# The next-to-last router's columns on VectorE, and that batch's scatters set around four small operations of the last batch

## The chip, the cores and the metric

The kernel runs on one core of one Trainium2 chip. The metric is the device time of that core in microseconds (us), as the median of several executions; lower is better. The engines are TensorE (PE, with its weight loads shown apart as PEld), VectorE (DVE), ScalarE (ACT), GpSimd (POOL) and SyncE (SP), which only issues transfers here. Each engine works through its own list of instructions in order, and they meet through semaphores: counters that one engine raises and another waits on.

## The reference

One transformer layer in fp32 on 8 batches of 512 tokens with 256 channels: attention, then a mixture of experts. Cut to what matters:

```python
x = x + attention(layernorm(x))          # 16 query heads, 4 key heads of 16, rope, causal
h = layernorm(x)                         # 4096 tokens
logits = h @ gate_w.T                    # 64 experts
topv, topi = jax.lax.top_k(logits, 8)
rw = softmax(topv)
gu = einsum('nh,eih->nei', h, gu_w);  gate, up = split(gu)
out = einsum('nei,ehi->nh', silu(gate) * up * W, dp_w)      # W holds rw at topi
out = out + sigmoid(h @ sh_gate1_w.T) * ((silu(h @ sh_gate_w.T) * (h @ sh_up_w.T)) @ sh_down_w.T)
x = x + out
```

## The kernel before, in words

The program has two phases. In the first, attention runs batch by batch, and each batch's tokens are routed and sent ("scattered") to the rows of a DRAM tensor `rows_d`, where every expert owns whole blocks of 128 rows. In the second, 320 such blocks are loaded (`xg<-rows_d`), put through their expert, scattered back to `res_d`, and summed per token. SP loads the first block only after all scatters of all batches have landed.

A batch is `b = h * 2 + par`, 0 to 7, and has four tiles of 128 tokens. The first phase is written as beats of 40 slots (`beat`, below); a beat holds the score and softmax work of one batch (`main`, eight units of five slots), and beside it work of its neighbours, each step put at a slot number. The slots only fix the order of the instructions in every engine's list: an engine that is early runs ahead until a semaphore stops it. The pieces around the change are:

- **`post`**, per tile: the attention output is turned, normalised by the softmax sums, projected, added to x, and its mean and variance are taken on DVE (L910, `mv`). At its step 2 POOL makes the reciprocal square root of the variance in two operations (L439 and L441, `rstd`), which the headline of the change calls a deviation. At step 4 DVE applies it (L916, `pay`), and then PE, ACT and DVE make logits and the top eight (L923 to L929).
- **`route`**, per batch, steps 0 to 11: counts of tokens per expert on PE, small column arithmetic on `col` (64 by 16) and the final row numbers `slot_i` (L322). The column arithmetic is `route_columns`: 3 instructions at step 0, 6 at step 2, one at step 4, 8 at step 5 and one at step 11, 19 in all. 12 of them are `chained`: the engine waits for its own result before it goes on. POOL runs them for batches 0 to 6, DVE for batch 7, the last. PE waits for `diag` (L310) before it makes the ranks (L668 to L678).
- **`scatter`**, per batch 32 times: one indirect transfer, issued by POOL (L457), that writes one row of 272 numbers for each of 128 tokens. The first one of a batch waits for `slot_i` and for the blank rows.
- **`ending(h, par, n)`** is true for the last n batches, two where n is left out.

The last three beats are: batch 7's main, beside which batch 6 goes through `post` and, at slots 29 to 39, through route steps 0 to 10, while batch 5's 32 scatters stand at slots 13 to 39; then a beat without main, in which batch 6's step 11 stands at slot 0, its scatters at slots 1 to 32, the end of batch 7's attention at slots 0 to 10, batch 7's `post` at slots 11 to 21 (its four deviations at slots 13 to 16) and its route from slot 22; then a beat with batch 7's step 11 and scatters. In the trace these are roughly 640 to 700 us, 700 to 760 us and 760 to 802 us.

## Time and profile before

| | |
|---|---|
| median of 3 executions | 1388.26 us (1385.78 to 1390.83) |
| the profiled execution, its own time | 1382.82 us |
| its span in the trace | 1381.0 us |
| busy share PE, DVE, ACT, POOL | 79%, 51%, 48%, 52% |
| mean granted TensorE clock | 0.903 of full |
| last scatter of the first phase ends | 801.9 us |

Times in the trace are microseconds from the start of its span. A row of a timeline gives the start, the busy time, the engine, the line of the kernel, the operation, what it writes and reads, how many instructions were merged, and in brackets how long the engine had been idle and what released it. "Remote" as the releaser means that no operation ended just then whose semaphore would explain it. "Issue" is time in which the engine waited for nothing that the profile shows. The names of line numbers are those of the kernel before; those of the changed kernel are 3 higher from L259 on.

### The profile page before, as it was taken

How to read it: one execution, taken by the hardware profiler on the slowest of the kernel's cores; microseconds unless marked ns; L12 is line 12 of the kernel's file. 1: busy time of each engine (PE TensorE's matmuls, PEld its weight loads, DVE VectorE, ACT ScalarE, POOL GpSimd, SP SyncE). 2: the span in 40 equal slices, each digit the busy share in tenths (PEclk: the TensorE clock that was granted, in tenths of full speed). 3: DMA queues.
4: the chain of work that ended last, by engine and by line, in shares of the span. 5: the costliest groups of instructions: out<-in, count | busy, mean ns of one | idle time of the engine just before them, and what ended most of it. 6: DMA issues, size and time to landing. Idle time of an engine off the chain costs nothing.

```text
span 1381.0 us, 24099 instructions
## 1 busy us (share of the span) xinstructions
PE 1085.1 (79%) x7306; PEld 835.8 (61%) x7306; DVE 708.3 (51%) x2229; ACT 661.8 (48%) x1650; POOL 722.3 (52%) x954
## 2 busy tenths in 40 slices
PE   3798998888888888889765068888879788788775
PEld 1566666655666656656533057777767677777663
DVE  3466766575666756666515411212244454544456
ACT  2466655555555555654421034544444454545441
POOL 3111225746557474564566745655556565565552
PEclk9699999899999999999867579989989999999996
DMA  2587876212122121231229765555767777766535
GB/s 82 174 283 226 279 253 230 99 39 101 63 70 107 39 97 57 66 104 61 84 85 314 252 191 168 170 161 158 233 218 275 262 274 239 273 237 216 199 108 207
DMA packets 142300, 233.22 MB, mean 169 GB/s; under 512 B 17287, under 2 KB 119894, under 8 KB 136800
## 3 DMA queue, kind: packets, MB, share of 16 engines
q1 hardware_dynamic: 67360, 101.06, 22.9%
q0 software_dynamic: 27648, 69.28, 14.1%
q10 hardware_dynamic: 47168, 61.35, 13.4%
q8 instruction: 63, 1.03, 0.3%
q14 instruction: 61, 0.50, 0.1%
HBM read 107.32 MB, written 132.66 MB: 174 GB/s over the span
## 4 chain that ended last, share of the span: by engine, by line
PE 47%; DVE 16%; another core or an unknown queue 14%; issue 11%; ACT 5%; POOL 3%; DMA 2%; ACTq 0%; DVEq 0%; SPq 0%; POOLq 0%
PE psB L1369 8%; PE psD L1386 6%; DVE nmax L866 6%; PE psv L601 4%; PE psA L1359 4%; PE ps L505 4%; PE ps L552 3%; PE psp L498 3%; PE psp L484 3%; PE ps L512 3%; PE psC L1377 2%; DMA x_d<-oT 2%; DVE acc L1201 1%; PE psq L628 1%
## 5 line engine op out<-in xcount | busy, mean ns | idle before, releaser
L1447 POOL DMA_INDIRECT res_d<-y,dst_i x320 | 322.6, 1008 | 230.5 <-ACT y L1275 127.6
L457 POOL DMA_INDIRECT rows_d<-pay,slot_i x256 | 256.2, 1001 | 76.0 <-issue 74.1
L866 DVE TENSOR_REDUCE nmax<-ps 128x1 f32<-128x512 f32 (+3 forms) x448 | 226.0, 531 | 132.2 <-PE ps L512 88.8
L732 ACT ACTIVATE wgu_s<-ps 128x512 f32<-128x512 f32 x320 | 191.9, 600 | 121.5 <-PE ps L512 90.2
L1178 DVE TENSOR_TENSOR inner<-inner,psB 128x128 f32<-128x128 f32 x160 | 45.9, 287 | 302.4 <-ACT inner L1262 221.8
L1369 PE MATMUL psB<-wgu_s,xT 128*128 x1280 | 182.4, 288 | 18.9 <-ACT xT L1255 12.3
L1386 PE MATMUL psD<-wdp_s,innerT 128*128 x640 | 176.5, 399 | 13.0 <-issue 7.6
L1369 PEld LDWEIGHTS psB<-wgu_s,xT 128*128 128x128 f32 x1280 | 166.1, 203 | 24.9 <-issue 24.8
L512 PE MATMUL ps<-mask,ident_b 128*128 128x256 bf16 (+1 forms) x640 | 174.7, 273 | 0.0
L505 PE MATMUL ps<-kT,qT 96*128 96x512 f32 (+3 forms) x512 | 168.2, 391 | 6.5 <-DVE nmax L866 3.3
L552 PE MATMUL ps<-qT,kT 128*128 128x512 f32 (+3 forms) x512 | 164.8, 385 | 4.5 <-ACT wgu_s L732 3.9
L1255 ACT COPY xT<-psA 128x512 f32<-128x512 f32 x160 | 97.1, 607 | 142.8 <-PE psA L1359 90.5
L1359 PE MATMUL psA<-cst,xg 128*128 128x128 f32 x640 | 104.0, 284 | 59.5 <-DMA xg<-rows_d 52.8
L1386 PEld LDWEIGHTS psD<-wdp_s,innerT 128*128 128x128 f32 x640 | 114.5, 200 | 29.9 <-issue 20.4
L1275 ACT COPY y<-psD 128x512 f32<-128x512 f32 x160 | 98.4, 615 | 68.3 <-remote 40.4
L1359 PEld LDWEIGHTS psA<-cst,xg 128*128 128x128 f32 x640 | 80.1, 148 | 61.4 <-DMA xg<-rows_d 53.7
L505 PEld LDWEIGHTS ps<-kT,qT 96*128 96x128 f32 x512 | 89.1, 203 | 32.2 <-DVE nmax L866 15.3
L512 PEld LDWEIGHTS ps<-mask,ident_b 128*128 128x128 bf16 x640 | 64.2, 100 | 64.7 <-issue 34.0
L1201 DVE SCALAR_TENSOR_TENSOR acc<-yk,rw_all,acc 128x256 f32<-128x256 f32 x204 | 98.8, 485 | 4.4
L1262 ACT ACTIVATE inner<-psB 128x128 f32<-128x128 f32 x160 | 48.4, 303 | 100.1 <-remote 66.5
L552 PEld LDWEIGHTS ps<-qT,kT 128*128 128x128 f32 x512 | 91.2, 205 | 7.4 <-ACT wgu_s L732 4.2
L601 PE MATMUL psv<-wgu_s 128*32 128x512 f32 (+3 forms) x1024 | 89.8, 470 | 3.7 <-issue 2.6
(257 smaller groups left out, 1606.3 us busy)
## 6 DMA issues: line engine op xcount, KB each, us to landing
rows_d<-blank ACTq DMA_DIRECT2D x8, 5440.0 KB, 19.3
xg<-rows_d SPq DMA_DIRECT2D x160, 272.0 KB
yk<-res_d SPq DMA_DIRECT2D x30, 1024.0 KB, 5.8
wgu_s<-wgu_in ACTq DMA_DIRECT2D x8, 1024.0 KB
x_d<-x SPq DMA_DIRECT2D x30, 192.5 KB
xs<-x_d SPq DMA_DIRECT2D x30, 192.5 KB
res_d<-y,dst_i POOLq DMA_INDIRECT x320
wgu_s<-x_in SPq DMA_DIRECT2D x32, 128.0 KB, 2.1
```

The costliest lines, as they stand in the source:

```text
L457: pool.indirect_dma_start(rows_d, bass.IndirectOffsetOnAxis(ap=slot_i[par][:, t, k:k + 1], axis=0), pay[par][:, t, :], None).then_inc(s_sc ...
L505: pe.matmul(ps1[:, bank, at:at + keys], qT[par][0:96, p, i * P:(i + 1) * P], kT[par][0:96, 2 * (p // 2) + ab, 0:keys], start=(at == 0), st ...
L512: return pe.matmul(blocks, ident_b[:], mask[:].unsqueeze(1).to_broadcast([P, blocks.shape[1], P]), start=False, stop=True, skip_group_chec ...
L552: pe.matmul(ps2[:, bank, at:at + n], kT[par][:, 2 * (p // 2) + ab, kt * P:(kt + 1) * P], qT[par][:, p, kt * P:SEQ], start=(at == 0), stop= ...
L601: last = pe.matmul(psv[32 * hh:32 * hh + 32, kt * P:SEQ], v1[par][:, kt, g, :], rhs, start=(kt == 0), stop=(kt == TILES - 1), skip_group_c ...
L732: act.activation(pexp[p % 4][:, s, :], ps2[:, (5 * p + s) % 2, :], ACT.Exp, scale=HEAD_D ** -0.5).then_inc(s_exp, 1)
L866: return dve.tensor_reduce(nmax[u][:, tile, heads[0]:heads[-1] + 1], src, AX.X, ALU.max, negate=True)
L1201: dve.scalar_tensor_tensor(out=acc[:, u], in0=yk_at(tile)[:, k], scalar=rw_all[:, at:at + 1], in1=xs_at(tile)[:, 0:D] if k == 0 else acc[: ...
L1359: last = pe.transpose(psA[:, i % 2, (b * KC + c) * P:(b * KC + c + 1) * P], xg[:, (2 * i + b) % G, c * P:(c + 1) * P], ident)
L1369: last = pe.matmul(psB[:, i % 2, b * GU:(b + 1) * GU], xT[:, i % A, b, c, :], wgu_s[:, bass.ds(off + c * GU, GU)], start=(c == 0), stop=(c ...
L1386: last = pe.matmul(psD[:, i % 2, b * D:(b + 1) * D], innerT[:, i % A, b, :], wdp_s[:, bass.ds(off, D)], start=True, stop=True)
L1447: pool.indirect_dma_start(res_d, bass.IndirectOffsetOnAxis(ap=dst_i[:, j % (2 * G):j % (2 * G) + 1], axis=0), y[:, j % Y, :], None, bounds ...
```

## The change

Two edits. The route columns of batch 6 go from POOL's list to DVE's, at the same slots (steps 0, 2, 5 and 11 ahead of what DVE already had there, step 4 behind it). And in the beat without main, batch 6's 32 scatters no longer stand one at each of the slots 1 to 32: twelve stand at slots 1 to 12, and twenty from slot 18 to slot 34, so that none stands at slots 13 to 17.

```diff
                     for n in range(TILES * TOP):
-                        if late and slot == first + n * spread // (TILES * TOP):
+                        at = first + n * spread // (TILES * TOP)
+                        if routed and behind:
+                            at = 1 + n if n < 12 else 18 + (n - 12) * 17 // (TILES * TOP - 12)
+                        if late and slot == at:
                             steps["scatter"](h - 1, par, n)
...
                 def route(h, par, k):
-                    if not ending(h, par, 1):
+                    if not ending(h, par):
                         route_columns(pool, h, par, k)
...
-                    if ending(h, par, 1) and k in (0, 2, 5, 11):
+                    if ending(h, par) and k in (0, 2, 5, 11):
                         route_columns(dve, h, par, k)
...
-                        if ending(h, par, 1):
+                        if ending(h, par):
                             route_columns(dve, h, par, k)
```

POOL's list before, from the end of batch 6's route columns to the end of the first phase (L457 is a scatter, L439 and L441 a deviation; the first seven scatters are batch 5's, and the last 48 are 16 of batch 6 and 32 of batch 7):

```order
L318 COPY col<-col 64x1
L457 DMA rows_d<-pay,slot_i 40960x272 x7
L322 TENSOR_SCALAR slot_i<-slot_f 128x32
L457 DMA rows_d<-pay,slot_i 40960x272 x13
L439 TENSOR_SCALAR rstd<-mv 128x1
L441 TENSOR_TENSOR rstd<-rstd,minus_half 128x1
L457 DMA rows_d<-pay,slot_i 40960x272
L439 TENSOR_SCALAR rstd<-mv 128x1
L441 TENSOR_TENSOR rstd<-rstd,minus_half 128x1
L457 DMA rows_d<-pay,slot_i 40960x272
```

POOL's list after, the same place (L460 is the scatter, L442 and L444 the deviation), from the last deviation of batch 6:

```order
L442 TENSOR_SCALAR rstd<-mv 128x1
L444 TENSOR_TENSOR rstd<-rstd,minus_half 128x1
L460 DMA rows_d<-pay,slot_i 40960x272 x32
L442 TENSOR_SCALAR rstd<-mv 128x1
L444 TENSOR_TENSOR rstd<-rstd,minus_half 128x1
L442 TENSOR_SCALAR rstd<-mv 128x1
L444 TENSOR_TENSOR rstd<-rstd,minus_half 128x1
L442 TENSOR_SCALAR rstd<-mv 128x1
L444 TENSOR_TENSOR rstd<-rstd,minus_half 128x1
L442 TENSOR_SCALAR rstd<-mv 128x1
L444 TENSOR_TENSOR rstd<-rstd,minus_half 128x1
L460 DMA rows_d<-pay,slot_i 40960x272 x52
```

Between batch 6's last deviation and batch 7's first, POOL now has 32 scatters in one row and nothing else: the last 20 of batch 5 and the first 12 of batch 6. Behind the four deviations stand 52, which are 20 of batch 6 and the 32 of batch 7; before, 3 stood between the deviations and 48 behind them.

DVE's list before, in the seventh unit of batch 7's main (L866 is a row maximum of the scores, L938 to L949 the parts of batch 6's route that DVE had):

```order
L938 TENSOR_TENSOR col<-psq,col 64x1
L866 TENSOR_REDUCE nmax<-ps 128x1
L941 TENSOR_REDUCE esum<-etop 128x4
L944 RECIPROCAL erec<-esum 128x4
L866 TENSOR_REDUCE nmax<-ps 128x1 x3
L947 TENSOR_TENSOR col<-psq,col 64x1
L949 TENSOR_TENSOR col<-psq,col 64x1
L866 TENSOR_REDUCE nmax<-ps 128x1 x2
L866 TENSOR_REDUCE nmax<-ps 128x2
```

And after, the later part of the same unit (L869 is the row maximum):

```order
L869 TENSOR_REDUCE nmax<-ps 128x1 x2
L311 TENSOR_TENSOR col<-col 64x1
L312 TENSOR_TENSOR col<-col 64x1
L313 TENSOR_TENSOR diag<-cst,col 64x192
L317 TENSOR_TENSOR col<-col 64x1
L318 TENSOR_SCALAR col<-col 64x1
L319 TENSOR_TENSOR col<-col 64x1
L320 COPY col<-col 64x1
L321 COPY col<-col 64x1
L869 TENSOR_REDUCE nmax<-ps 128x2
```

Eight instructions of the columns now stand ahead of that unit's last maximum. Six more stand behind the same unit's first maximum, three ahead of the last maximum of the unit before, one behind L952 (step 4), and one (step 11) behind all of batch 7's maxima.

## Rows read from the trace of the kernel before

**Rows 1.** The page's first line, and the chain that ended last: start, us, what
```profile
span 1381.0 us, 24099 instructions
...
711.14 12.04 another core or an unknown queue
...
803.47 2.50 DMA xg<-rows_d
```

**Rows 2.** Timelines of PE and ACT, end of batch 7's attention
```profile
691.71 0.48 PE L668 MATMUL psq<-diag,ones_f 64*128 64x128 f32 x2 [2.33 <-POOL diag L310]
...
704.42 0.59 ACT L759 COPY oT<-psv 128x512 f32<-128x512 f32 x1 [4.73 <-remote]
...
711.76 4.50 PE L601 MATMUL psv<-wgu_s 128*32 128x512 f32 x32 [0.69 <-ACT wgu_s L732]
...
723.21 0.59 ACT L759 COPY oT<-psv 128x512 f32<-128x512 f32 x1 [11.49 <-remote]
```

**Rows 3.** Timeline of POOL, 667 to 704 us: batch 5's scatters and batch 6's columns
```profile
667.81 1.09 POOL L457 DMA_INDIRECT rows_d<-pay,slot_i  x1 [0.19 <-issue]
...
679.85 0.97 POOL L457 DMA_INDIRECT rows_d<-pay,slot_i  x1 [0.30 <-issue]
683.65 0.19 POOL L295 TENSOR_SCALAR col<-col 64x1 f32<-64x1 f32 x1 [2.83 <-DVE col L938]
...
693.23 0.18 POOL L318 COPY col<-col 64x1 f32<-64x1 f32 x1 [0.16 <-POOL col L317]
694.22 1.26 POOL L457 DMA_INDIRECT rows_d<-pay,slot_i  x1 [0.81 <-POOL col L318]
...
703.12 0.34 POOL L322 TENSOR_SCALAR slot_i<-slot_f 128x32 int32<-128x32 f32 x1
```

**Rows 4.** Timeline of DVE, 678 to 700 us: batch 7's row maxima
```profile
678.60 0.76 DVE L866 TENSOR_REDUCE nmax<-ps 128x1 f32<-128x384 f32 x2 [4.36 <-remote]
682.29 0.69 DVE L866 TENSOR_REDUCE nmax<-ps 128x2 f32<-128x512 f32 x1 [2.94 <-remote]
...
699.72 0.17 DVE L881 TENSOR_TENSOR mt<-nmax,mt 128x8 fp32r<-128x8 f32 x1
```

**Rows 5.** Timeline of POOL, 704 to 801 us: the scatters of batches 6 and 7
```profile
704.62 1.06 POOL L457 DMA_INDIRECT rows_d<-pay,slot_i  x1 [1.16 <-issue]
...
720.01 0.97 POOL L457 DMA_INDIRECT rows_d<-pay,slot_i  x1 [0.30 <-issue]
730.41 0.22 POOL L439 TENSOR_SCALAR rstd<-mv 128x1 f32<-128x1 f32 x1 [9.42 <-DVE mv L910]
...
737.51 0.57 POOL L441 TENSOR_TENSOR rstd<-rstd,minus_half 128x1 f32<-128x1 f32 x1
738.27 1.22 POOL L457 DMA_INDIRECT rows_d<-pay,slot_i  x1 [0.19 <-issue]
...
757.75 0.96 POOL L457 DMA_INDIRECT rows_d<-pay,slot_i  x1 [0.30 <-issue]
761.66 0.96 POOL L457 DMA_INDIRECT rows_d<-pay,slot_i  x1 [2.95 <-issue]
...
800.96 0.96 POOL L457 DMA_INDIRECT rows_d<-pay,slot_i  x1 [0.30 <-issue]
```

**Rows 6.** Timeline of DVE, 735 to 760 us: batch 7's post and route
```profile
735.16 0.18 DVE L910 BATCH_NORM_AGGREGATE mv<-stat 128x2 f32<-128x6 f32 x1
...
738.12 0.41 DVE L916 TENSOR_SCALAR pay<-oT,mv,rstd 128x256 f32<-128x256 f32 x1 [1.93 <-POOL rstd L441]
...
744.00 0.15 DVE L297 TENSOR_SCALAR col<-col 64x1 f32<-64x1 f32 x1
744.30 0.15 DVE L298 TENSOR_TENSOR col<-col 64x1 f32<-64x1 f32 x1
744.38 0.20 DVE L299 TENSOR_SCALAR col<-col 64x1 f32<-64x1 f32 x1
...
759.26 0.18 DVE L322 TENSOR_SCALAR slot_i<-slot_f 128x32 int32<-128x32 f32 x1 [2.92 <-remote]
```

## The prediction

> **What bounds the kernel now.** I read the page first, then the chain that ended last, then the timelines of single engines around the place of the change. The span is 1381.0 us [rows 1]; the profiled execution took 1382.82 us and the median is 1388.26, so I add what the change does to the span onto both. The changed lists differ only from 676 us on and up to the end of the first phase, where the first expert block is loaded at 803.47 [rows 1]. All work behind that load is the same and starts when the last scatter has landed, so the change is worth what it does to the end of POOL's 32 scatters of batch 7, whose last one starts at 800.96 [rows 5]. They run at a fixed pace: 31 steps from 761.66 to 800.96 are 1.27 us each [rows 5]. So the question is when the first of them starts, now 761.66.
>
> Back from there: POOL finishes batch 6's scatters at 757.75 + 0.96 = 758.71, then takes 2.95 us to start batch 7's first [rows 5]. About 1.16 of that is POOL going through the waits of a batch's first scatter, as at 704.62 [rows 5]; the other 1.8 are a real wait for `slot_i`, which DVE makes at 759.26 [rows 6]. That comes from DVE's chain of batch 7's post, which starts when ACT copies the last attention output at 723.21, after 11.49 us without work [rows 2]. This is the largest idle piece, and the chain shows it as 12.04 us without a known cause [rows 1]: PE's products began at 711.76 and the modelled end is 716.26, yet ACT is released 7 us later [rows 2].
>
> The rows show a pattern for it. POOL issues 13 scatters without a pause from 704.62 to 720.98 [rows 5], and ACT is released 2.2 us after the last. The previous copy waited 4.73 us and was released at 704.42 [rows 2], 1.3 us after POOL ended a row of seven scatters at 703.1 [rows 3]. DVE's maxima at 678.60 and 682.29 waited 4.36 and 2.94 us [rows 4], the second until 1.5 us after the scatter of 679.85 to 680.82, behind which POOL paused [rows 3]. In each case a finished operation's signal reaches the waiting engine late while scatters run back to back, and soon after they stop. I take that as the working reading: **long unbroken rows of scatters hold up the signals of the other engines**. The trace doesn't show why.
>
> **The columns leave POOL.** In 667 to 703 us POOL had pauses in which it waited for DVE's and PE's parts of the route, for instance the 2.83 us before 683.65 and the stretch from 683.65 to 693.23 [rows 3]. With the 19 instructions gone, nothing stands between batch 5's scatters: the order shows 20 of batch 5 in one row from 667.81 [rows 3]. They end at 667.81 + 19 x 1.27 + 0.96 = 692.9 instead of 703.1. That by itself gains nothing, since the next scatter waits for batch 6's `slot_i`, which is now DVE's. But it makes one unbroken row of 25 us where there were pauses.
>
> **The columns arrive at DVE**, among batch 7's maxima. On DVE a chained step takes 0.30 us (744.00 to 744.30) and one without a wait 0.08 (744.30 to 744.38) [rows 6]. 12 x 0.30 + 7 x 0.1 = 4.3 us. Of it some hides in DVE's waits for PE between maxima; bounds 0 and 4.3, and I take half, 2.2, as nothing speaks for either end. The Trainium skill (VectorE: DVE Perf Modes, Rules for kernel authors) says to "minimize op *count*, not sems", because the pipeline empties after each operation anyway. By it the waits would be free and 19 operations of 0.15 to 0.20 us would cost about 3.3; the two pitches above contradict it, a wait costs 0.2 us here, and the sum goes by the rows. On the other side PE no longer waits 2.33 us for POOL's `diag` at 691.71 [rows 2], because DVE makes it two slots ahead; I take the 2.3 off.
>
> Ten slots of maxima lie between 682.29 and 699.72 [rows 4]: 17.4 us, without the 2.3 it is 15.1, with DVE's 2.2 it is 17.3, 1.73 a slot. Under a row of scatters the two slots before took from 674.24 (678.60 less its wait) to 682.29, 4.0 each [rows 4]. Now the row goes on to 692.9, and signals are held to about 694.2. That is 11.9 us at 4.0, three slots. The other seven take 12.1, so the maxima end at 706.3 and not 699.9: **6.4 us later**. Bounds: nothing held, 699.6; nothing moves at all until 694.2, 711.5.
>
> **Batch 6's `slot_i` and its first twelve.** POOL made `slot_i` at 703.12 [rows 3], after its seven scatters; DVE now makes it at 706.4. The first scatter starts 1.5 us behind that start, as 704.62 behind 703.12, at 707.9, and the twelfth ends 11 x 1.27 + 0.96 = 14.9 later, at 722.8. Batch 7's last products need, from 699.9 to their modelled end at 716.26, 16.4 us of which about 4 were held (the 4.73 of [rows 2]); so they are done near 718.7. Their signal is held until the twelve are through, plus 1.3 to 2.2 as measured above: 724.1 to 725.0. ACT's copy moves from 723.2 to about 724.5, **1.3 later**. So the shift of 6.4 is mostly absorbed, because the old row of 13 ended at 721.0 and the new row of 12 ends at 722.8.
>
> **The four deviations kept clear.** The last mean and variance is ready at 735.16 + 0.18 = 735.34, and POOL's deviation for it ended at 737.51 + 0.57 = 738.08, behind interleaved scatters; DVE waited 1.93 us for it at 738.12 [rows 5, 6]. Without them it takes 0.2 + 0.9 us, so it ends at 736.4, and DVE's chain and `slot_i` come up to 1.7 earlier. But POOL then has 20 scatters of batch 6 left, where it had 16: they end at 736.6 + 19 x 1.27 + 0.96 = 761.7, against 758.71 [rows 5]. `slot_i` (near 757.6) is then waiting for POOL and not POOL for it. Batch 7's first scatter starts at 761.7 + 1.16 = 762.9, **1.2 later** than 761.66. POOL's 9.42 us of idleness before 730.41 [rows 5] stays unused, and one more scatter than before is on its wrong side. Bounds: 1.2, and 3.0 if `slot_i`'s signal is itself held to the end of the row, as at 759.26 (2.92 us, [rows 6]), when the old gap of 2.95 returns.
>
> Sum: 1.3 + 1.2 = +2.5 us. The profiled execution would take 1385.3, the median 1388.26 + 2.5 = **1390.8**.
>
> **Rivals.** (a) *Nothing is held during the 20.* The first 7 us of the row from 704.62 passed without a hold, as the products could begin at 711.76 [rows 2, 5], so a long row need not hold always. Then the maxima end at 699.6, the twelve scatters run from about 701.2 to 716.1, ACT's copy comes at 717.4 to 718.3, 5.3 earlier, and with the 1.2 the total is -4.1: 1384.2. Against it stand the waits of [rows 4] under only ten scatters. (b) *The maxima are late but the last products' signal is not held*, since they end at 718.7 in the middle of a row: -4.5 + 1.2 = -3.3, 1385.0. Against it stand both copies of [rows 2]. (c) *Slower: under the 20 almost nothing moves.* DVE now waits for its own results 12 times inside the row, and each can be caught like the 2.92 us before 759.26 [rows 6]. The maxima end at 711.5, the twelve run from 713.1 to 728.0, the copy comes at 729.3 to 730.2, 6.5 later, and with 1.2 to 3.0 the total is +7.7 to +9.5: 1396 to 1398. Since batch 6's scatters start from DVE, each us by which the maxima end beyond 706.3 costs one; it becomes visible when they end later than about 708. (d) *The second edit does what it says and is worth its 1.7 us:* only if POOL is through before `slot_i` comes, and 736.6 + 25.1 against 757.6 says it isn't; where copy and post come early, all of this moves together.
>
> **How the numbers follow.** Chances: the forecast 0.50, (a) 0.20, (b) 0.12, (c) 0.18. A measurement of this kernel can tell about 0.3%, 4.2 us, from no change. The forecast lies inside it, but its bounds (the hold, and the 3.0) put 0.08 of its 0.50 beyond; (c) is beyond, slower; of (a) half is beyond, faster, and of (b) a sixth. Faster 0.15, within 0.59, slower 0.26. The range takes in (a) and (b) with some scatter below, and (c) but for its far end: 1383.5 to 1397.
>
> **What would show it.** After: batch 5's scatters end near 693; batch 7's maxima end near 706, with DVE waits of 2 to 5 us marked remote before 694; DVE's `slot_i` for batch 6 directly behind; ACT's last copy within 1 to 2 us after the twelfth scatter; no wait of DVE for `rstd`; 52 scatters behind the deviations with only some 1.2 us between the 20th and the 21st; the first block loaded near 806. If the maxima end near 700 and the copy comes near 718, (a) is right; if they end beyond 710, (c). The prediction is wrong in kind if ACT's copy isn't tied to the end of the scatters, or if POOL waits for batch 7's `slot_i` again.

## The result, and the profile after

The changed kernel takes 1401.13 us (median of 6 executions, 1395.51 to 1405.85), the kernel before takes 1387.16 beside it (6 executions, 1380.30 to 1390.83). The ratio is 1.0094, with a 95% interval of 1.0067 to 1.0120: **0.9% slower**, where I had forecast 0.2%, inside what can be told from no change, and a range up to 1397.0. The profiled execution took 1400.32 us with a span of 1398.5, against 1382.82 and 1381.0 [rows 1]. One execution of all that are reported here, of 1677.67 us at a granted clock of 0.554 in experiment 12, was in a slower state of the chip and is left out of its ratio.

The first lines that answer to [rows 1]: the page's first line, then from the chain that ended last (start, us, what) the piece that is longest in the disputed stretch, and the load of the first expert block.

```profile
span 1398.5 us, 24099 instructions
...
682.45 15.21 another core or an unknown queue
...
819.32 2.66 DMA xg<-rows_d
```

The load starts 15.85 us later than at 803.47 [rows 1], so nearly all of the 17.5 us of the span arise before it. The timeline of POOL (start, us, engine, line, operation, what is written from what, and in brackets the idle time before it and who ended it) shows the rows of scatters. Every row starts or ends with one of these lines; left out are scatters at the same pitch and the four deviations.

```profile
669.93 1.09 POOL L460 DMA_INDIRECT rows_d<-pay,slot_i  x1 [0.19 <-issue]
...
694.09 0.96 POOL L460 DMA_INDIRECT rows_d<-pay,slot_i  x1 [0.30 <-issue]
716.67 0.96 POOL L460 DMA_INDIRECT rows_d<-pay,slot_i  x1 [21.61 <-issue]
...
730.58 0.96 POOL L460 DMA_INDIRECT rows_d<-pay,slot_i  x1 [0.30 <-issue]
...
748.05 1.09 POOL L460 DMA_INDIRECT rows_d<-pay,slot_i  x1 [0.18 <-issue]
...
772.18 0.96 POOL L460 DMA_INDIRECT rows_d<-pay,slot_i  x1 [0.30 <-issue]
777.61 0.96 POOL L460 DMA_INDIRECT rows_d<-pay,slot_i  x1 [4.46 <-issue]
```

The row of twenty of batch 5 starts at 669.93, where the kernel before had 667.81 [rows 3]: at this point, ahead of anything that the change touches, this execution is already 2.1 us late. I take that off below. The rows of scatters are as forecast: twenty in 25.1 us, twelve in 14.9, twenty in 25.1. What is not as forecast is what the other engines do under them. DVE, from the first row of twenty to batch 7's `slot_i`:

```profile
681.42 0.75 DVE L869 TENSOR_REDUCE nmax<-ps 128x1 f32<-128x384 f32 x2 [5.05 <-remote]
...
697.69 0.69 DVE L869 TENSOR_REDUCE nmax<-ps 128x2 f32<-128x512 f32 x1 [15.24 <-remote]
...
699.37 0.14 DVE L298 TENSOR_SCALAR col<-col 64x1 f32<-64x1 f32 x1
699.65 0.15 DVE L299 TENSOR_SCALAR col<-col 64x1 f32<-64x1 f32 x1
...
715.21 0.17 DVE L884 TENSOR_TENSOR mt<-nmax,mt 128x8 fp32r<-128x8 f32 x1
715.33 0.18 DVE L325 TENSOR_SCALAR slot_i<-slot_f 128x32 int32<-128x32 f32 x1
...
747.90 0.47 DVE L919 TENSOR_SCALAR pay<-oT,mv,rstd 128x256 f32<-128x256 f32 x1 [0.46 <-POOL rstd L444]
...
761.84 0.15 DVE L319 TENSOR_TENSOR col<-col 64x1 f32<-64x1 f32 x1 [1.19 <-DVE col L318]
...
770.49 0.42 DVE L969 TENSOR_TENSOR place<-psq,thd 128x256 f32<-128x256 f32 x1 [4.60 <-issue]
...
775.90 0.18 DVE L325 TENSOR_SCALAR slot_i<-slot_f 128x32 int32<-128x32 f32 x1 [2.86 <-remote]
```

And ACT at the same three places: an exponential under the first row, the last attention output behind the twelve, and batch 7's route under the second row of twenty.

```profile
698.39 0.60 ACT L735 ACTIVATE wgu_s<-ps 128x512 f32<-128x512 f32 x1 [14.91 <-PE ps L515]
...
733.76 0.59 ACT L762 COPY oT<-psv 128x512 f32<-128x512 f32 x1 [11.75 <-remote]
...
770.19 0.27 ACT L800 COPY thd<-psq 128x128 f32<-128x128 f32 x1 [16.21 <-remote]
```

The waits of 4.36 and 2.94 us of [rows 4] have become 5.05 and 15.24. The second stands until 2.6 us after the row's last scatter ends (694.09 + 0.96 = 695.05), and ACT stands still over the same time. PE's timeline under the row (xcount is the number of matmuls in a line), and at its end the products of batch 7's last attention step:

```profile
681.95 0.44 PE L515 MATMUL ps<-mask,ident_b 128*128 128x256 bf16 x1
...
682.88 2.36 PE L604 MATMUL psv<-wgu_s 128*32 128x384 f32 x16
...
688.47 0.48 PE L604 MATMUL psv<-wgu_s 128*32 128x128 f32 x2 [1.82 <-issue]
689.90 0.37 PE L604 MATMUL psv<-wgu_s 128*32 128x128 f32 x1 [0.95 <-issue]
691.30 0.44 PE L604 MATMUL psv<-wgu_s 128*32 128x128 f32 x2 [1.03 <-issue]
692.73 0.37 PE L604 MATMUL psv<-wgu_s 128*32 128x128 f32 x1 [0.99 <-issue]
694.14 0.78 PE L508 MATMUL ps<-kT,qT 96*128 96x512 f32 x1 [1.04 <-issue]
...
722.06 2.36 PE L604 MATMUL psv<-wgu_s 128*32 128x512 f32 x32 [0.69 <-issue]
```

Two different things can be seen here.

**The work is done and its signal comes late.** The maximum at 697.69 waits for one product alone, the one at 681.95, whose modelled end is 682.39: 15.3 us pass between the two. ACT's exponential at 698.39 waits for a product with the modelled end 682.95. ACT's last copy waits for the products that start at 722.06 and have the modelled end 724.42; it is at 733.76, 2.2 us after the last of the twelve, as that of 723.21 [rows 2] came 2.2 us after the thirteenth. The trace also records the updates of the semaphores. The one of those last products is recorded at 733.74, directly ahead of the copy, so the delay lies ahead of the update, and not between the update and ACT.

**PE crawls.** The 24 products from 682.88 on are one group, and the kernel has no wait ahead of any of them. Yet from the seventeenth on they come one or two at a time every 0.7 to 2.1 us, 10.2 us for all (682.88 to 693.10), with idle time marked "issue". I had read only DVE, ACT and POOL at such places before. So "signals are held" is half of it: **under the long row an engine's own instructions can come slowly too**. But DVE's and ACT's waits here aren't that crawl, since the products that they need stand ahead of the 24.

Between 753.98 and 770.19 ACT waits again, for a product whose modelled end is 762.62. Before that, DVE is slow in batch 7's route: a step that had a pitch of 0.30 us at 699.37 has an idle time of 1.19 ahead of it at 761.84. Each of these steps waits for the signal of DVE's own step before.

### The profile page after: what moved, and what is told of

The parts are those of the page before. It is cut to its first block, busy times and chain, and to the rows that moved or that the text cites. A ratio compares the mean times of both kernels' runs of the same rounds, so it can differ in the third digit from the quotient of the medians.

```text
span 1398.5 us, 24099 instructions
## 1 busy us (share of the span) xinstructions
PE 1095.6 (78%) x7306; PEld 844.4 (60%) x7306; DVE 711.2 (51%) x2248; ACT 663.9 (47%) x1650; POOL 715.6 (51%) x935
## 3 DMA queue, kind: packets, MB, share of 16 engines
q0 software_dynamic: 27648, 69.28, 13.9%
q10 hardware_dynamic: 47168, 61.35, 13.3%
## 4 chain that ended last, share of the span: by engine, by line
PE 52%; DVE 16%; issue 14%; another core or an unknown queue 11%; ACT 3%; POOL 2%; DMA 1%; SPq 0%; ACTq 0%; DVEq 0%; POOLq 0%
PE psB L1372 9%; PE psD L1389 7%; DVE nmax L869 6%; PE psA L1362 4%; PE psv L604 4%; PE ps L508 3%; PE ps L555 3%; PE psp L501 3%; PE psp L487 3%; PE psC L1380 3%; PE ps L515 3%; PE psq L631 1%; PE ps L549 1%; DVE acc L1204 1%
## 5 line engine op out<-in xcount | busy, mean ns | idle before, releaser
L460 POOL DMA_INDIRECT rows_d<-pay,slot_i x256 | 253.8, 992 | 97.6 <-issue 97.3
L869 DVE TENSOR_REDUCE nmax<-ps 128x1 f32<-128x512 f32 (+3 forms) x448 | 225.5, 530 | 146.5 <-PE ps L515 88.0
L1372 PE MATMUL psB<-wgu_s,xT 128*128 x1280 | 185.1, 291 | 15.3 <-issue 8.6
L1389 PE MATMUL psD<-wdp_s,innerT 128*128 x640 | 179.0, 402 | 17.3 <-ACT innerT L1271 8.2
L1389 PEld LDWEIGHTS psD<-wdp_s,innerT 128*128 128x128 f32 x640 | 116.4, 203 | 35.4 <-issue 25.7
L515 PEld LDWEIGHTS ps<-mask,ident_b 128*128 128x128 bf16 x640 | 64.1, 100 | 64.9 <-issue 36.5
```

Of the source, the lines that this page charges most:

```text
L460: pool.indirect_dma_start(rows_d, bass.IndirectOffsetOnAxis(ap=slot_i[par][:, t, k:k + 1], axis=0), pay[par][:, t, :], None).then_inc(s_sc ...
L515: return pe.matmul(blocks, ident_b[:], mask[:].unsqueeze(1).to_broadcast([P, blocks.shape[1], P]), start=False, stop=True, skip_group_chec ...
L869: return dve.tensor_reduce(nmax[u][:, tile, heads[0]:heads[-1] + 1], src, AX.X, ALU.max, negate=True)
L1372: last = pe.matmul(psB[:, i % 2, b * GU:(b + 1) * GU], xT[:, i % A, b, c, :], wgu_s[:, bass.ds(off + c * GU, GU)], start=(c == 0), stop=(c ...
L1389: last = pe.matmul(psD[:, i % 2, b * D:(b + 1) * D], innerT[:, i % A, b, :], wdp_s[:, bass.ds(off, D)], start=True, stop=True)
```

## Experiments

**The theories.** Theory 1 is the working reading of the prediction: a long unbroken row of POOL's scatters holds up the other engines (their signals, as I put it; by the rows above their instructions too), and the change made such rows. Theory 2: the harm is the work that DVE got, 19 operations with 12 waits on itself among the maxima. Theory 3, in the first two experiments: the second edit made the loss. Ratios are always to the kernel before, run in between on the same chip. They aren't the quotients of the medians. Each run bears the number of its chip: experiments 1 to 4 ran on chip 0 (kernel before 1389.52 us), 5, 6, 8 and the first kernel of 9 on chip 5 (1366.53), the second run of the changed kernel, 7, 10 and the second kernel of 9 on chip 8 (1365.60), 11 on chip 1 (1211.39) and 12 on chip 11 (1212.16). The chip of the result above (1387.16) isn't on record. Times of different chips can't be compared, ratios can with care; chips 1 and 11 turned out to matter by themselves, and I call them the quick chips.

**1. The columns alone.** The kernel before, with one condition changed at its three places:

```diff
-                    if not ending(h, par, 1):
+                    if not ending(h, par):
```

> The first edit alone: batch 6's columns on DVE, the scatters at their old slots. Theory 1 (the unbroken row of 20 scatters holds up the other engines' signals while batch 7's maxima run): DVE has one wait of over 10 us inside that row, the maxima end some 13 us later than before, and the kernel is 7 to 12 us slower than before. Theory 2 (DVE's added work and its own waits among the maxima cost it): the same time, but without a wait of over 5 us; the delay lies in the slots that hold the columns. Theory 3 (the second edit made the loss, by 20 scatters behind the deviations): within 3 us of before.

Measured: 1399.35 us, 1.0079 (1.0043 to 1.0116). DVE in this kernel, under a row of twenty from 668.81 to 693.9:

```profile
679.66 0.76 DVE L866 TENSOR_REDUCE nmax<-ps 128x1 f32<-128x384 f32 x2 [4.41 <-remote]
...
697.28 0.69 DVE L866 TENSOR_REDUCE nmax<-ps 128x2 f32<-128x512 f32 x1 [16.56 <-remote]
```

The first edit alone gives most of the loss and the same hold as the changed kernel: the maximum's product has its modelled end at 680.52, 16.8 us ahead of 697.28.

**2. The scatters' slots alone.** The kernel before with the other edit:

```diff
+                        if routed and behind:
+                            at = 1 + n if n < 12 else 18 + (n - 12) * 17 // (TILES * TOP - 12)
```

> The second edit alone: the columns stay on POOL, twelve scatters of batch 6 ahead of the four deviations and 20 behind. In the changed kernel the stretch from ACT's last copy of the attention output to the end of the last scatter grew by 5.3 us. Theory 1: this is the second row of 20 holding batch 7's route, so this kernel is 3 to 6 us slower than before. Theory 2: only POOL's later end counts, +1.2 us. Theory 3: 10 us slower or more.

Measured: 1389.86 us, 1.0024 (0.9990 to 1.0059). There is no row of twenty among the maxima, but 52 scatters now stand in one row from 742.89 to 808.74, and under it ACT's copy for the route waits:

```profile
761.45 0.27 ACT L800 COPY thd<-psq 128x128 f32<-128x128 f32 x1 [12.62 <-remote]
```

What the second edit costs is too small to be told from nothing by the interval. The stretch from ACT's last copy to batch 7's first scatter, which grew by 5.4 us in the changed kernel, is 40.38 us here and 38.45 in the kernel before. That is 1.9 more, not the 5.3 that theory 1 was given.

**3. The columns on DVE, POOL's waits kept.** Edit 1, and POOL goes through batch 6's waits for the route as before, without doing the arithmetic. That keeps pauses between its scatters.

```diff
+                    elif not ending(h, par, 1):
+                        for at, sem_, count in ((0, s_top, 4 * (b + 1)), (2, s_cnt, b + 1), (4, s_erec, b + 1),
+                                                (5, s_base, b + 1), (5, s_pool, 12 * (b + 1)), (11, s_slot, b + 1)):
+                            if k == at:
+                                pool.wait_ge(sem_, count)
...
```

> As cols_only, but POOL keeps the waits of batch 6's route (for the top eights, the counts, the reciprocal sums, the bases, the end of the columns and the slots) at their old places, without the arithmetic; so batch 5's scatters have pauses again while DVE does exactly the work of cols_only. Theory 1: no row of 20, no wait of over 6 us, within 4 us of before. Theory 2: as slow as cols_only, since DVE's list is the same.

Measured: 1391.78 us, 1.0032 (1.0000 to 1.0063). DVE's list is that of experiment 1. Its waits at the disputed place are near those of the kernel before again, 3.65 and 3.23 us. But the pauses now end where DVE is quick, and 7 scatters of batch 5 and 13 of batch 6 stand in one row from 699.39 to 724.71:

```profile
684.62 0.76 DVE L873 TENSOR_REDUCE nmax<-ps 128x1 f32<-128x384 f32 x2 [3.65 <-remote]
689.01 0.69 DVE L873 TENSOR_REDUCE nmax<-ps 128x2 f32<-128x512 f32 x1 [3.23 <-remote]
```

```profile
723.62 0.59 ACT L766 COPY oT<-psv 128x512 f32<-128x512 f32 x1 [17.16 <-remote]
```

Theory 1 had expected no wait over 6 us; with the new row there is one all the same. The hold went with the row, not with the work: from DVE's maxima to ACT's copy.

**4. The changed kernel, its scatters paced.** In batch 7's main part POOL waits, ahead of each scatter, for the maxima of two slots before its own:

```diff
+                            if PACED(h, par, main):
+                                steps["pace"](h, par, slot)
...
+                def pace(h, par, slot):
+                    pool.wait_ge(s_red, 5 * PAIRS_OF_HEADS * (h * 2 + par) + slot - 1)
```

> The changed kernel with one thing more: in the beat with batch 7's main, each scatter of POOL first waits for the row maxima of two slots before, so that POOL can't run ahead of DVE and stops when DVE stops. Theory 1: POOL's stopping ends each hold, no DVE wait of over 5 us there, the maxima end 8 us or more sooner than in the changed kernel, and the total is 3 to 7 us over before (the second edit's share stays). Theory 2: as slow as the changed kernel, 12 to 14 us over before, since DVE's list is the same and POOL's is later.

Measured: 1390.36 us, 1.0017 (0.9987 to 1.0046). The row of twenty is now one of ten, one of two, one of six and two single ones; the longest remote wait of DVE there is 4.32 us. From the start of batch 5's twenty scatters to the end of the maxima it takes 35.4 us (677.48 to 712.92), where the changed kernel has 45.5 and the kernel before 32.1. Most of the loss is gone, with all of DVE's new work in place. The row of twenty behind the deviations is still there, and ACT still waits 22.05 us for it at 773.14.

**5. DVE's work alone.** The kernel before, in which DVE does 19 spare operations of the same kinds, with the same chain of 12 waits on itself, at the same places, while POOL does its own as before. Three of them are smaller than those of the change, as the expectation says. A part of one of the five pieces:

```diff
+                if k == 2:
+                    chained(eng.tensor_scalar(c(5), c(4), P / 2 - 0.5, 1.0 / P, ALU.add, ALU.mult), 1)
+                    chained(eng.tensor_scalar(c(5), c(5), 1.0, None, ALU.add), 2)
+                    chained(eng.tensor_scalar(c(6), c(5), 1.0, 0.5, ALU.add, ALU.mult), 3)
+                    eng.tensor_tensor(c(7), c(6), c(1), ALU.subtract)
...
```

> The kernel before, and beside it 19 operations of the kind and order of the columns on DVE, at the places where the change puts them, on spare tiles with their own chain of 12 waits (the wide one writes 64 by 128 bf16 instead of 64 by 192 fp32, and two of the three small ones bf16); nobody waits for them, and POOL's list is the old one. It prices DVE's added work alone. Theory 1: at most 4 us slower than before, most likely 1 to 3. Theory 2 (DVE's work is what costs): 8 us or more slower.

Measured: 1366.39 us, 1.0016 (0.9992 to 1.0040). The upper end is 5.5 us, the middle 2.2, and nothing at all lies inside the interval too (the quotient of the medians is 0.9999). Theory 2 can't give the 0.9% of the change.

**6. The changed kernel with pauses.** Ahead of batch 5's scatters 12, 16, 20, 24 and 28 POOL does five chained memsets of a spare tile, 2.5 us in all from the end of one scatter to the start of the next.

```diff
+                    if isinstance(b, int) and b == BATCH - 3 and n >= 12 and n % 4 == 0:
+                        for again in range(5):
+                            pool.memset(spare[:], 0.0).then_inc(s_spare, 1)
+                            pool.wait_ge(s_spare, 5 * (n // 4 - 3) + again + 1)
...
```

> The changed kernel, with five pauses of POOL of some 2 us each in the row of 20 scatters (ahead of batch 5's scatters 12, 16, 20, 24 and 28), made of five small memsets of a spare tile, so by time alone and not by a wait for another engine. Theory 1 in the form that a pause of POOL ends a hold: no hold over 8 us in that row, the maxima end 5 us or more sooner than in the changed kernel, total 3 to 9 us over before. If holds need more than a pause, or what counts is the number of scatters in some longer time, the hold stays near 15 us and so does the loss.

Measured: 1364.13 us, 0.9982 (0.9957 to 1.0007). **POOL does more, and the kernel is faster.** I had expected 3 to 9 us over the kernel before, and it is not slower at all. In the rows of four no wait of DVE is above 1.4 us and none of ACT above 3.0. The changed kernel without pauses once more, now on chip 8, whose kernel before takes 1365.60 us against the 1366.53 of chip 5:

> The changed kernel once more, beside the next three on one chip. Both theories: 1.006 to 1.012 times the kernel before, POOL's row of 20 scatters, DVE's wait of about 15 us inside it, maxima ending 8 to 10 us late.

Measured: 1379.28 us, 1.0084 (1.0051 to 1.0118). Against that the pauses give back 1.0%, all of the 0.84% that was lost; the comparison is between two chips, each with its own kernel before. Its DVE and ACT under the row of twenty (663.27 to 688.42):

```profile
687.40 0.69 DVE L869 TENSOR_REDUCE nmax<-ps 128x2 f32<-128x512 f32 x1 [12.93 <-remote]
691.88 0.69 DVE L869 TENSOR_REDUCE nmax<-ps 128x1 f32<-128x512 f32 x1 [3.22 <-remote]
```

```profile
690.92 0.60 ACT L735 ACTIVATE wgu_s<-ps 128x512 f32<-128x512 f32 x1 [15.60 <-remote]
```

Here PE's 24 products are through at 682.32, and the product that the maximum of 687.40 waits for has its modelled end at 675.67, 11.7 us ahead of it. From ACT's last copy to batch 7's first scatter it is 39.59 us in this execution, where the one above has 43.85.

**7. Rows of eight.** The same with pauses ahead of scatters 12, 20 and 28 only (`n in (12, 20, 28)`), on chip 8 as well.

> The changed kernel with three pauses, before batch 5's scatters 12, 20 and 28, so rows of eight where rows of four gave 0.9982. If the hold grows with the length of the row from about the fifth scatter on: two waits of DVE or ACT of 3 to 6 us, one in each row of eight, and 1.001 to 1.004. If only rows of 10 and more hold: no wait above 2.5 us there and the 0.998 of the rows of four. If the harm is DVE's work: 1.006 or more, whatever the rows.

Measured: 1365.70 us, 0.9994 (0.9968 to 1.0019). The first row of eight, 661.48 to 671.42, has a wait; the second, 673.87 to 683.69, has none on DVE above 1.4 us:

```profile
672.87 0.69 DVE L876 TENSOR_REDUCE nmax<-ps 128x2 f32<-128x512 f32 x1 [6.09 <-PE ps L522]
679.55 0.76 DVE L876 TENSOR_REDUCE nmax<-ps 128x1 f32<-128x384 f32 x2 [1.17 <-PE ps L522]
```

So eight in a row can hold up DVE, and need not. I had expected a hold in each, or in none. The name of the releaser is PE's matmul here and not "remote", but the end of the wait, 1.45 us after the end of the row, is the same.

**8. A gate for the last products.** The kernel before, and POOL waits for the last attention products ahead of batch 6's seventh scatter. That breaks the row of thirteen of [rows 5] at the place where ACT's last copy is due:

```diff
+                    if n == 6 and isinstance(b, int) and b == BATCH - 2:
+                        pool.wait_ge(s_pv, KV_HEADS * BATCH)
```

> The kernel before, with one wait more: POOL stops after six of batch 6's scatters until PE's last product of attention is in. Theory 1: the row of 13 that held this signal for 7 us becomes a row of 6; ACT's last copy comes 4 to 6 us earlier, and the seven scatters left fit into the 9.4 us that POOL idled before the first deviation, so the kernel is 3 to 6 us faster than before. If the hold of that signal has another cause (PE's products really last so long), no change, or a loss of 2 to 4 us through the later scatters.

Measured: 1360.90 us, **0.9955 (0.9933 to 0.9977), faster than both kernels**. POOL and ACT there:

```profile
711.68 0.97 POOL L459 DMA_INDIRECT rows_d<-pay,slot_i  x1 [0.30 <-issue]
716.92 0.97 POOL L459 DMA_INDIRECT rows_d<-pay,slot_i  x1 [4.28 <-PE psv L603]
```

```profile
716.68 0.59 ACT L761 COPY oT<-psv 128x512 f32<-128x512 f32 x1 [4.32 <-PE psv L603]
```

Where the kernel before had 11.49 us and "remote" [rows 2], ACT waits 4.32 us for the matmul that really ends then. POOL gives up 4.28 us of its row and gets more back. There is a second gain that I hadn't expected: batch 7's route, from its first step on DVE to `slot_i`, takes 10.3 us (737.77 to 748.08), where the kernel before took 16.9 (742.59 to 759.44) and the changed one 22.6 (753.53 to 776.08), although 48 scatters follow each other under it from 733.46 on:

```profile
737.77 0.18 DVE L285 TENSOR_TENSOR etop<-topv 128x32 f32<-128x32 f32 x1
...
747.90 0.18 DVE L322 TENSOR_SCALAR slot_i<-slot_f 128x32 int32<-128x32 f32 x1
```

So a long row need not hold anything. The three other kernels with the gate in experiments 9 and 10 show the same (9.7 to 10.2 us); the ten traces without it on chips 0, 5 and 8 and on the chip of the result have 13.9 to 25.7. Theory 1 in the form "a row of that length holds" is too simple.

**9. More pacing on top.** The gate together with the pacing of experiment 4 in batch 7's main part, and with the pacing in every main part:

> The kernel before with the wait of before_pv and with the pacing of after_paused (in the beat with batch 7's main each scatter waits for the row maxima of two slots before). Theory 1: both holds shorter, 4 to 9 us faster than before. If pacing only moves scatters to where they hold something else, no better than before_pv.

> The kernel before with POOL's scatters in every main part tied to DVE's progress (each waits for the maxima of the slot before its own), and the wait for the products before batch 6's seventh. If unbroken rows are the harm throughout the attention: below the 0.9955 of the one wait alone, 0.985 to 0.993. If only the row at the last copy matters: 0.995 to 0.997. If each wait of POOL costs more than the rows: above 0.998.

Measured: 1362.79 us, 0.9965 (0.9938 to 0.9993), and 1361.04 us, 0.9976 (0.9952 to 0.9999). Neither is better than the gate alone. In the second the row from 659.80 to 668.49 still has holds up to 3.5 us: a wait for two slots before (the code is that of experiment 4, the expectation names one slot) doesn't break a row that POOL is late with.

**10. All together.** The columns on DVE, the scatters' old slots, the pauses of experiment 6, and the gate:

> The columns on DVE, batch 5's scatters broken into rows of four by pauses, POOL's wait for the products before batch 6's seventh scatter, and the old slots of the scatters. If unbroken rows are the whole harm: at or below the kernel before with the same wait alone (0.9955), so 0.992 to 0.996, the maxima ending 1 to 3 us earlier than in the kernel before. If DVE's extra work costs the 2.2 us of the prediction: 0.997 to 0.999. If the columns on DVE are themselves the harm: above 1.003.

Measured: 1359.17 us, 0.9955 (0.9932 to 0.9977), the ratio of the gate alone. With the rows broken the columns on DVE neither cost nor give anything that can be told.

**11. What about the row does it?** Three forms of the changed kernel in which batch 5's scatters 12 to 31 give way to something else, and follow in a row ahead of batch 6's first. In place of each: three chained memsets; a scatter of the first 64 rows; a plain transfer of 128 rows.

```diff
+                        for again in range(3):
+                            pool.memset(spare[:], 0.0).then_inc(s_spare, 1)
+                            pool.wait_ge(s_spare, 3 * (n - 12) + again + 1)
```

```diff
+                        pool.indirect_dma_start(
+                            rows_d, bass.IndirectOffsetOnAxis(ap=slot_i[par][0:64, t, k:k + 1], axis=0),
+                            pay[par][0:64, t, :], None).then_inc(s_first, 16)
```

```diff
+                        pool.dma_start(spare_d[:, n - 12, :], pay[par][:, t, :]).then_inc(s_first, 16)
```

> The changed kernel with POOL busy but not scattering in the disputed stretch: in place of each of batch 5's scatters 12 to 31 three chained memsets (about 1.4 us), and the twenty scatters themselves in a row ahead of batch 6's first. The reference's output; the whole is longer by about the 25 us of that row, so only the stretch of batch 7's maxima is read. If it is the scatters that hold the signals: no remote wait of DVE or ACT above 2.5 us there, and the maxima take 20 us or less from the first of the ten slots on. If it is POOL being busy without a pause, whatever it does: holds of 10 us and more as in the changed kernel.

> In the disputed stretch batch 5's scatters 12 to 31 move only the first 64 of their 128 rows; all of their 128 rows are sent again in a row ahead of batch 6's first scatter, so the output is the reference's and only the stretch of the maxima is read. If the hold grows with the rows that are in flight: shorter than the changed kernel's 13 to 15 us, at most half of it. If it goes by the number of scatters in a row: 10 us and more again, provided that POOL issues them at the same 1.27 us; where it issues them faster, until the end of a shorter row.

> In the disputed stretch POOL sends plain transfers of the same 128 rows to a fixed place in its slots 12 to 31, and the indirect scatters come in a row ahead of batch 6's first; the output is the reference's and only the stretch of the maxima is read. If POOL's transfers of any kind hold the signals: waits as in the changed kernel. If only the indirect ones do (each row to an address of its own): no remote wait above 2.5 us.

Measured: 1231.65, 1229.59 and 1232.44 us, one execution each, against **1211.39 for the kernel before**. No wait of DVE or ACT was held in any of the three, but not even under the full scatters ahead of and behind the stretch, for instance a row of 8 from 618.57 to 628.53. On this chip nothing is held, so the three kernels don't answer the question.

**12. The change where nothing is held.** Instead they opened a better test: the same kernels where theory 1 has nothing to work on. All fell on a chip of that kind again, chip 11 (the kernel before takes 1212.16 us).

> The changed kernel once more, whichever chip it falls on. The last three runs fell on one on which the kernel before takes 1211.39 us and no wait of DVE or ACT in rows of 8 and of 32 full scatters, nor in 20 half ones, was above 2 us. If the harm is the hold alone: on such a chip (before near 1211) 0.997 to 1.001, since the maxima then end where DVE's work puts them; on one where the kernel before takes 1365 to 1390, 1.006 to 1.012 again. If the harm is the change's own work: 1.006 to 1.012 on any chip.

> The kernel before with POOL's one wait for the last products. If its gain is the hold taken away: on a chip without holds 0.999 to 1.005, since the wait then only delays scatters; on one where the kernel before takes 1365 to 1390, 0.993 to 0.998 again.

> POOL busy with chained memsets in place of batch 5's scatters 12 to 31, which follow in a row ahead of batch 6's first; only the stretch of the maxima is read. On a chip where the changed kernel's maxima are held for 13 to 15 us: no remote wait above 2.5 us there if it is the scatters that hold, 10 us and more if it is POOL being busy. On a chip without holds it tells nothing more than before.

Measured: **the changed kernel 1207.59 us, 0.9959 (0.9945 to 0.9974): faster than before**; the gate 1210.62 us, 1.0000 (0.9986 to 1.0014). The memsets once more took 1231.01 us in one execution and add nothing. The changed kernel here: the row of twenty on POOL, DVE and ACT under it, and ACT's last copy under the twelve.

```profile
633.42 1.09 POOL L460 DMA_INDIRECT rows_d<-pay,slot_i  x1 [0.19 <-issue]
...
657.88 0.96 POOL L460 DMA_INDIRECT rows_d<-pay,slot_i  x1 [0.30 <-issue]
663.23 0.96 POOL L460 DMA_INDIRECT rows_d<-pay,slot_i  x1 [4.39 <-issue]
```

```profile
639.77 0.75 DVE L869 TENSOR_REDUCE nmax<-ps 128x1 f32<-128x384 f32 x2
...
641.63 0.69 DVE L869 TENSOR_REDUCE nmax<-ps 128x2 f32<-128x512 f32 x1 [0.80 <-PE ps L515]
...
655.59 0.69 DVE L869 TENSOR_REDUCE nmax<-ps 128x1 f32<-128x512 f32 x1 [1.34 <-PE ps L515]
...
661.77 0.17 DVE L884 TENSOR_TENSOR mt<-nmax,mt 128x8 fp32r<-128x8 f32 x1
```

```profile
673.50 0.59 ACT L762 COPY oT<-psv 128x512 f32<-128x512 f32 x1 [4.61 <-PE psv L604]
```

The two maxima that waited 5.05 and 15.24 us wait for nothing and for 0.80 us. The second starts 0.04 us after the modelled end of its product at 641.31, where 15.3 us passed before, and PE's same 24 products take 1.50 us where they took 10.2:

```profile
641.31 0.28 PE L515 MATMUL ps<-mask,ident_b 128*128 128x256 bf16 x1
...
641.83 1.50 PE L604 MATMUL psv<-wgu_s 128*32 128x384 f32 x24
```

The row of twenty is as unbroken and as fast as ever (25.4 us), and the copy comes in the middle of the row of twelve, which ends at 678.1. In the kernel with the gate, which keeps the columns on POOL, the same maxima on this chip end at 662.32:

```profile
662.32 0.17 DVE L883 TENSOR_TENSOR mt<-nmax,mt 128x8 fp32r<-128x8 f32 x1
...
671.59 0.59 ACT L761 COPY oT<-psv 128x512 f32<-128x512 f32 x1 [2.48 <-PE psv L603]
```

Both kernels start their last scatter ahead of the row of twenty at 631.0. So the columns on DVE end the maxima 0.5 us earlier here, as rival (a) had it. The rest isn't as (a) had it. The gate never stops POOL on this chip (its thirteen scatters run in one row from 667.38 to 683.72), so this trace has the order of the kernel before. Against it the last copy of the changed kernel comes 1.9 us later, and the last scatter of the first phase ends at 752.73 where it ends at 752.59 with the gate: in these two executions the change gains nothing ahead of the first expert block. For the same reason the 1.0000 of the gate says little: here the wait does nothing.

**What a chip without holds is worth.** The two traces of the changed kernel, on the chip of the result and on chip 11, have the same 24,099 instructions in the same order, so they can be laid side by side by the number of a matmul:

| matmul of PE, counted from 0 | result's chip, us | chip 11, us | later by |
|---|---|---|---|
| 1157, just behind the first scatter at 214.70 | 215.15 | 214.67 | 0.5 |
| 1434 | 261.02 | 253.98 | 7.0 |
| 1689 | 300.05 | 293.21 | 6.8 |
| 3977, under the first scatters of the row of twenty | 670.20 | 633.68 | 36.5 |
| 4064 | 700.54 | 645.65 | 54.9 |
| 4306, the first of the second phase | 822.11 | 757.24 | 64.9 |
| 7305, the last | 1391.23 | 1203.31 | 187.9 |

Up to POOL's first scatter the two agree within 0.5 us. Between 261 and 300 us, where only eight scatters stand and no row is longer than five, nothing is added. All the rest is added in stretches in which POOL scatters, and most of it in the second phase, which this document doesn't take apart.

A second difference goes with the first. Before 200 us both traces record about the same number of semaphore updates (1441 and 1447); in all it is 11,375 on the result's chip and 21,202 on chip 11. Under the row of twenty the semaphore of batch 5's scatters has 64 recorded updates on the one and 336 on the other, and a scatter raises it by 16. The count has to be reached for the kernel to go on, so it is records that are missing. Every trace on chips 0, 5 and 8 has 10,890 to 11,506 updates, every one on chips 1 and 11 has 21,191 to 21,511. With it "remote" is partly a word for a missing record. It also names a rival that no run here tested: that it is the recording of the traces itself, under the load of the scatters, that holds the engines on some chips. Each execution here comes with a traced span, so none is free of it.

## Why the prediction was wrong, point by point

The place was right and so was the kind of mechanism. The step that failed is the price of the hold under the row of twenty: one term of the sum was sized wrong by a factor of two (6.4 us, measured 13.4), and the cost of the second row of twenty was left out of it.

- **The row of twenty, and DVE's 19 operations: right.** 25.1 us as forecast. Chained steps have a pitch of 0.28 us (699.37 to 699.65) where I had 0.30. From the held maximum to the end of the maxima I had 17.3 us for ten slots; it is 715.21 + 0.17 - 697.69 = 17.7. The 2.2 us taken for DVE is what experiment 5 has in the middle of its interval, which takes in 0 as well.
- **"11.9 us at 4.0, three slots": this step failed.** I took the pace of two slots under a row of ten as the pace under any row. In fact no maximum moved after 682.17: DVE waited 15.24 us and went on at 697.69, 2.6 us after the row. From [rows 4]'s 682.29 to this 697.69, less the 2.1 of the start, that is 13.3 us, and the maxima end 13.4 later instead of 6.4. The rival (c) had this ("under the 20 almost nothing moves"), and was 1.8 us short, since the hold outlasted the row by 2.6 and not by the 1.3 that I had from two short rows, and the ten slots took 17.7 and not 17.3. Experiments 1, 3, 4 and 6 show that the row does it and not DVE's waits on itself, which (c) had named as the cause. A pace for a slot was the wrong unit: one signal, raised at a modelled end of 682.39, came through at 697.69, after the row. In the kernel before, the same product ends at 680.31, and the row of ten ended at 680.82 [rows 3]; its maximum is at 682.29, 2.0 us behind the product. The 4.0 us a slot that I read there were the end of a short row. The same holds for PE's 24 products, which came just after that row:

```profile
680.79 2.61 PE L601 MATMUL psv<-wgu_s 128*32 128x384 f32 x24
```

  In the changed kernel PE had to take all of them inside the row. That they cost time of their own isn't shown, since the maximum ahead of them was held longer.
- **The row of twelve and the copy: right in kind.** First scatter 1.3 us behind `slot_i` (forecast 1.5), the copy 2.2 us behind the twelfth (1.3 to 2.2). As I had written, each us of the maxima beyond 706.3 costs one: the copy comes 733.76 - 723.21 - 2.1 = 8.4 us later, not 1.3. The old hold absorbs 5 of the 13.4.
- **The four deviations: the gain is there, its price was half seen.** The wait for `rstd` is 0.46 us instead of 1.93. But the row of twenty behind them holds batch 7's own route. I had that only as a bound of 3.0 for `slot_i`'s signal. From the copy to batch 7's first scatter it was 38.45 us and is 43.85: **5.4 more, where the sum had 1.2**. ACT's 16.21 us and DVE's slow chain inside that row are the rest: the route takes 22.6 us, where it takes 9.8 on chip 11 (692.37 to 702.13). The 5.4 is of one execution: the same stretch is 40.38 in experiment 2 and 39.59 in the second run of the changed kernel, 1.9 and 1.1 over the 38.45, so the 1.2 of the sum isn't refuted as the usual cost. Under the first row I had priced every slot; under the second I priced one signal, and as a bound only.
- **The sum.** 8.4 + 5.4 = 13.8, with the 2.1 that this execution was late at the start 15.9, which is 777.61 - 761.66. The 2.1 is no effect of the change that I can show: the median of the ratio is 1.0094, 13.0 us, near the 13.8.
- **The chances.** (c) had 0.18 and happened, with the row as its cause and not DVE's waits on itself. (a), "nothing is held during the 20", had -4.1 us, and on chip 11 the change measures -4.6 us by the medians. But (a) has the copy 5.3 us earlier, and there it comes 1.9 later than with the inert gate, at the same end of the first phase. So the agreement of that number is luck as far as the traces show, and where the 4.6 us come from stays open. I had weighed the two as rivals for one answer, and which of them is nearer depends on where the kernel runs. The chances were also added wrongly: by their own terms it is faster 0.12 and within 0.62, not 0.15 and 0.59.

**Shown**: on chips 0, 5 and 8 the loss goes with the unbroken rows (experiments 3, 4, 6, 10 with the same work on DVE; 1 with a row of twenty), the gate in the row of thirteen gains 0.45% on chip 5, of which the trace shows both places (the copy and the route), and on chip 11, where nothing is held, the loss is gone. **Open**: what holds the engines up. That it needs something beyond this kernel is all that the quick chips tell; whether that is the chip, what else runs on it or the recording of the trace, and whether it is the rows in flight, the kind of transfer or POOL being busy, no run here could tell. One candidate has a row against it: the fetching of instructions. Under the row of twenty one of its two queues moved one packet of 16 KB at 680.34 in 0.95 us, no slower than its others in this trace (0.88 to 2.16 us), and the other moved none. Nor is it settled how long a row must be: in experiments 6 and 7 rows of four gave nothing above 3.0 us, rows of eight 6.09 us once and nothing the other time, and with the row of eight that the kernel before has from 645.93 to 655.88 goes a wait of ACT of 7.28 us, until 657.51; the rows of ten to twenty in the changed kernel and in experiments 1, 3, 4, 6, 7 and 10 held, and the rows of 48 behind the gate of experiments 8 to 10 did not. What the gate changes for a row that starts 17 us later isn't known, and it wasn't tried separately. Nor does a hold always last until the row ends: in the rows of 52 of experiments 2, 6 and 7 and of the second run of the changed kernel, ACT's waits of 11.8 to 13.2 us end 17.7 to 19.2 us behind the start of the row, with more than 45 us of scatters still to come.

## What to carry to other kernels

When a trace has waits marked "remote", or idle time marked "issue" between instructions that wait for nothing, and they end soon after a row of GpSimd's indirect transfers, give the row pauses at the places where other engines' signals are due, by a wait on just those signals; here one such wait gained 0.45% on a chip that holds, and on one that doesn't it never stopped POOL. Taking work off an engine that issues such transfers isn't free: its waits were the pauses. Before calling a wait a held signal, or a slow engine its cause, find the one instruction that is waited for and compare its end: here PE did crawl, and what DVE and ACT waited for stood ahead of the crawl. And a duration read under a short row must not be stretched over a longer one; price it from both sides, with "nothing moves at all" as a full case; it had 0.18 here and happened. And where a trace lacks records, lay it beside one that has them: the first place where the two drift apart names the suspect.

## What the runs showed of the hardware that I had not expected

- Under rows of 20 scatters at a pitch of 1.27 us PE took single matmuls every 0.7 to 2.1 us with nothing to wait for, DVE its chained steps at up to 1.39 us instead of 0.30 (760.45 to 761.84), a product's signal came up to 16.8 us behind its modelled end (experiment 1), and ACT waited up to 22.05 us, part of it for late work (experiment 4). Most waits over 10 us ended between 1 us before and 3.4 us after the end of the row; four under rows of 52 ended well inside.
- "Another core or an unknown queue" in a chain can be a signal of the same core that comes late: the chain gives 15.21 us from 682.45 to it, and the product that DVE waited for all that time has its modelled end at 682.39.
- The same program takes 1387.16, 1389.52, 1366.53 and 1365.60 us as a median on four occasions and 1212.16 on chip 11. The granted TensorE clock of the profiled executions (0.895 to 0.911 on the former, 0.920 to 0.932 on the quick chips) differs by 1 to 4%, the time by 11 to 13%. The two traces part where POOL's first indirect transfer stands, at 214.70 us. The chains that ended last can't be compared: the page of the kernel before gives 14% of its span, about 190 us, to "another core or an unknown queue", but the chain of the changed kernel on chip 11 starts only at 738.82 us and says nothing of the first phase.
- A verdict on a change can turn round with the chip: 1.0094 and 1.0084 on two, 0.9959 on another.
